# Block sums over two slots, packed rows for the rotary attention, and ScalarE writing the normalised rows, in a fused two-layer decoder

## The reference, cut to what matters

```
x = LN(x + taylor_attention(x));  x = LN(x + wide_cross_attention(x, ctx))      # layer 0
x = LN(x + gelu_experts(x))
x = LN(x + causal_attention(x))       # 16 heads of 8, softmax(q k / sqrt(8) + slopes) v, then Wo
x = LN(x + rotary_cross_attention(x, ctx))   # 16 heads of 8, q and k RMS-normed and rotated, 77 keys
x = LN(x + swiglu_experts(x))
```

## Time and profile before

| what | value |
|---|---|
| median of three runs | 2771.97 us |
| profiled execution | 2773.75 us |
| its trace's span | 2772.0 us |
| PE busy | 2534.0 us (91%) |
| DVE busy | 1904.9 us (69%) |
| ACT busy | 1671.0 us (60%) |
| POOL busy | 1694.9 us (61%) |
| DMA, one core's 16 engines | 97 GB/s mean |

### The profile page before, as it was taken

The page is one execution under the profiler, slowest core; times in us unless marked ns, Lnnn a source line. Parts: engine busy times, 40 slices in busy tenths (PEclk is TensorE's granted clock), DMA queues, the critical chain, the costliest instruction groups (busy, mean ns, idle before and its releaser), DMA issues. The chain is left out here.

```text
span 2772.0 us, 61590 instructions
## 1 busy us (share of the span) xinstructions
PE 2534.0 (91%) x19168; PEld 1864.5 (67%) x19168; DVE 1904.9 (69%) x5298; ACT 1671.0 (60%) x4543; POOL 1694.9 (61%) x2110
## 2 busy tenths in 40 slices
PE   8998999999999289996999999969999999699996
PEld 6665887877877289993555555547766666458993
DVE  6884677787777355555777777765788886445655
ACT  6773666666665234444766666639888887623334
POOL 3442334555555645554888888846688887724675
PEclk9998999999999699998999999979999999899998
DMA  8932467777774122214100000000011010011336
GB/s 260 338 107 68 151 215 226 234 224 224 223 220 129 54 65 71 72 58 129 58 11 9 9 11 9 7 25 13 16 30 30 30 30 17 30 30 54 93 93 194
DMA packets 274799, 267.86 MB, mean 97 GB/s; under 512 B 30060, under 2 KB 253561, under 8 KB 274096
## 3 DMA queue, kind: packets, MB, share of 16 engines
q1 hardware_dynamic: 256912, 228.42, 27.2%
q0 software_dynamic: 17280, 34.13, 3.6%
q10 hardware_dynamic: 288, 1.38, 0.2%
HBM read 101.24 MB, written 151.85 MB: 91 GB/s over the span
## 5 line engine op out<-in xcount | busy, mean ns | idle before, releaser
L779 POOL TENSOR_TENSOR wide_probs<-wide_exps,wide_inv_sum 128x616 f32<-128x616 f32 x128 | 168.3, 1315 | 305.6 <-DVE wide_inv_sum L1580 293.0
L749 POOL TENSOR_TENSOR causal_exps<-causal_biased,causal_neg_max 128x512 f32<-128x512 f32 x256 | 262.8, 1036 | 76.4 <-DVE causal_neg_max L1594 76.2
L758 POOL DMA_INDIRECT sorted_x<-send,place_i x240 | 244.1, 1017 | 84.2 <-ACT send L1233 44.0
L1289 ACT ACTIVATE rotary_exps<-banks,rotary_neg_max 128x77 f32<-128x77 f32 x1024 | 248.7, 341 | 19.3 <-DVE rotary_neg_max L1594 19.1
L1764 POOL DMA_INDIRECT results<-gelu_tile_out,gelu_dest_i x142 | 140.1, 986 | 142.2 <-DVE gelu_tile_out L1920 120.0
L1539 DVE TENSOR_TENSOR causal_biased<-banks,regions 128x512 f32<-128x512 f32 x256 | 163.6, 680 | 80.7 <-PE banks L1115 80.4
L1764 POOL DMA_INDIRECT results<-swiglu_tile_out,swiglu_dest_i x142 | 144.6, 1019 | 116.7 <-DVE swiglu_tile_out L1915 59.4
L1833 ACT ACTIVATE gelu_hidden<-banks,gelu_slot 128x256 f32<-128x256 f32 x284 | 116.6, 470 | 159.5 <-PE banks L2010 159.4
L1258 ACT ACTIVATE causal_exps<-causal_exps 128x512 f32<-128x512 f32 x256 | 161.2, 630 | 71.4 <-POOL causal_exps L749 71.4
L1594 DVE TENSOR_REDUCE rotary_neg_max<-banks 128x4 f32<-128x308 f32 x256 | 121.7, 475 | 113.5 <-PE banks L1129 105.1
L1273 ACT ACTIVATE causal_probsT<-banks 128x512 f32<-128x512 f32 x256 | 151.6, 592 | 79.3 <-PE banks L1140 79.3
(11 more groups left out here) (385 smaller groups left out, 7018.3 us busy)
## 6 DMA issues: line engine op xcount, KB each, us to landing
v_dram<-wide_staged SPq DMA_DIRECT2D x38, 1024.0 KB, 4.4
sorted_x<-blank SPq DMA_DIRECT2D x1, 34848.0 KB, 116.8
sorted_x<-blank SPq DMA_DIRECT2D x24, 1452.0 KB, 8.7
wide_folded<-v_dram SPq DMA_DIRECT2D x128, 256.0 KB
gelu_tile_in<-sorted_x SPq DMA_DIRECT2D x71, 132.0 KB, 2.1
swiglu_tile_in<-sorted_x SPq DMA_DIRECT2D x71, 132.0 KB, 2.1
gelu_back<-results SPq DMA_DIRECT2D x16, 512.0 KB, 8.0
swiglu_back<-results SPq DMA_DIRECT2D x16, 512.0 KB, 5.4
```

Source lines behind the costliest of these rows:

```text
L749: pool.tensor_tensor(exps[:, (NU * pair.c + m) % ES], biased[:, m % BS].rearrange("p (h n) -> p h n", h=HU), neg_max[:, m % SLOTS].unsquee ...
L758: pool.indirect_dma_start(route["sorted_x"], bass.IndirectOffsetOnAxis(ap=r_place_i[:, b % 2, which, n // 2:n // 2 + 1], axis=0), send[:, ...
L779: pool.tensor_tensor(probs[:, half % SLOTS, 0:HH * NK].rearrange("p (k h) -> p h k", h=HH), exps[:, half % EB], inv_sum[:, half % SLOTS].u ...
L1289: last = act.activation(exps[:, (NU * c.c + k) % ES, h], scores[:, h * NK:(h + 1) * NK], ACT.Exp, bias=neg_max[:, k % SLOTS, h:h + 1])
```

## The change

Line numbers in this section's order rows are those of the kernel they come from.

1. **Sums.** `late_sum`, four matmuls in each slot, becomes `late_sums` (causal) and `dense_sum` (rotary), eight matmuls in every second slot. In the causal stage the block stands right behind the score matmuls of even slots, PLAG is 5 instead of 4, and `probsT` has 4 buffers instead of 2.
2. **Rotary packed.** The exponentials of two slots (8 heads x 77 keys = 616 columns) lie side by side in a buffer of 640 columns. Five transposes of 128 columns take the place of eight of 77, and ACT copies 256 and 384 columns instead of 512 and 512. The values must then lie as 616 rows: they are made four pairs ahead (a third part of `early`), written by ACT to `v_rows` in SBUF, stored to DRAM by four DMAs and loaded to `v_dense` by five, for each pair. `v_rows` has one buffer; ACT waits until the store of the pair before has landed.
3. **Output chain.** In the causal stage the output transpose, copy and product come two to three slots later (OT_LAG 3, `turn_outputs` in slot 1 of the next step), the division in slots 5 and 6 instead of 4 and 6, and POOL adds the residual in slot 6 and makes `rstd` in slot 5.
4. **LN.** POOL computes shift = -mean x rstd (two instructions on 128x2), and ACT writes X as z x rstd + shift: two instructions of 128x128 a pair, in both stages, instead of DVE (causal) and POOL (rotary).
5. The context ring of the rotary stage has 4 buffers instead of 8.

```diff
-    FU = {"wide": 7, "causal": 4, "rotary": 2}[kind]
+    FU = {"wide": 7, "causal": 4, "rotary": 1}[kind]
-    EARLY = 2
+    EARLY = 3
+    PITCH, HALF_ROWS = 320, 8 * CONTEXT
-    OT, OT_LAG = (1, 1) if kind == "causal" else (2, 0)
+    OT, OT_LAG = (1, 3) if kind == "causal" else (2, 0)
...
+            def store_values(pair):
+                sp.wait_ge(early_done, pair.count(EARLY, EARLY))
+                rows = route["v_dram"][4 * HALF_ROWS * pair.c:4 * HALF_ROWS * (pair.c + 1)].rearrange("(m h k) c -> h k m c", h=4, k=NK)
+                for h in range(4):
+                    sp.dma_start(rows[h], v_rows[0:NK].rearrange("k (m r) -> k m r", r=PITCH)[:, :, 64 * h:64 * h + 64]
+                                 ).then_inc(v_stored, 16)
+            def load_values(pair):
+                s = pair.c % 2
+                sp.wait_ge(v_stored, 16 * 4 * (pair.c + 1))
+                if pair.c >= 2:
+                    sp.wait_ge(pv_done, pair.back(2).count(NU, NU))
+                for b in range(2):
+                    for n in range(2):
+                        at = HALF_ROWS * (2 * (2 * pair.c + b) + n)
+                        sp.dma_start(v_dense[:, s, b, n, 0:4], route["v_dram"][at:at + 512].rearrange("(c p) d -> p c d", p=P)).then_inc(v_loaded[s], 16)
...
-                    if c is not None and kind != "rotary" and k == 3:
+                    if c is not None and kind != "rotary" and k == (6 if kind == "causal" else 3):
...
-                    if n is not None and kind == "rotary" and k in (3, 4):
-                        pool.tensor_scalar(X[:, n.index(2, b), :], z[:, s, b], mean_var[:, s, b, 0:1], rstd[:, s, b:b + 1],
+                        if late:
+                            pool.wait_ge(rstd_done, n.count(1, 1))
+                            pool.tensor_tensor(shift[:, s], mean_var[:, s, :, 0], rstd[:, s], ALU.mult).then_inc(turned_done, 1)
+                            pool.wait_ge(turned_done, n.count(1, 1))
+                            pool.tensor_scalar(shift[:, s], shift[:, s], -1.0, None, ALU.mult).then_inc(shift_done, 1)
...
+            if m == 4:
+                if f.c >= 1:
+                    act.wait_ge(v_stored, 16 * 4 * f.c)
+                return act.activation(v_rows[0:NK].rearrange("p (m w) -> p m w", w=PITCH // 4)[:, :, 0:D],
...
-        EARLY_AT = [(0, 0), (1, 0)]
+        EARLY_AT = [(0, 0), (1, 0), (7, 0)]
-        TLAG, PLAG, OLAG = {"wide": (4, 5, 6), "causal": (3, 4, 5), "rotary": (2, 3, 4)}[kind]
+        TLAG, PLAG, OLAG = {"wide": (4, 5, 6), "causal": (3, 5, 5), "rotary": (2, 3, 4)}[kind]
+        DIVIDE_AT = (5, 6) if kind == "causal" else (4, 6)
...
+            def late_sums(pair, n):
+                b, g = n // UB, n % UB // 2
+                pe.wait_ge(probsT_done, pair.count(NU, n + 1))
+                for odd in range(2):
+                    for h in range(HU):
+                        last = pe.matmul(o_bank[b][32 * h:32 * h + 32, g * P:(g + 1) * P], values[:, pair.c % 2, strip:strip + 32],
+                                         probsT[:, (n - 1 + odd) % 4, h * P:(h + 1) * P], start=odd == 0, stop=odd == 1)
...
+            def dense_sum(pair, n):
+                b, g, s = n // UB, n // 2 % 2, pair.c % 2
+                pe.wait_ge(probsT_done, pair.count(NU, n + 1))
+                for second in range(2):
+                    for strip in range(4):
+                        chunk = strip + second
+                        last = pe.matmul(o_bank[b][32 * strip:32 * strip + 32, g * P:(g + 1) * P],
+                                         v_dense[:, s, b, g, chunk, 32 * (strip % 2):32 * (strip % 2) + 32],
+                                         probsT[:, (NU * pair.c + n) // 2 % 2, chunk * P:(chunk + 1) * P], start=second == 0, stop=second == 1)
...
+                    if kind == "rotary" and mine is not None and k == 4:
+                        s = mine.c % 4
+                        act.wait_ge(shift_done, mine.count(1, 1))
+                        for b in range(2):
+                            act.activation(X[:, mine.index(2, b), :], z[:, s, b], ACT.Identity, bias=shift[:, s, b:b + 1],
+                                           scale=rstd[:, s, b:b + 1]).then_inc(x_written, 1)
```

180 lines of the change are left out of this document (118 added, 62 removed).

## The result

| | before | after |
|---|---|---|
| median of the runs, us | 2770.5 (4 runs, 2765.8 to 2773.2) | 2740.0 (4 runs, 2739.0 to 2740.8) |
| ratio, 95% interval | | 0.9892 [0.9877, 0.9907] |
| profiled execution: span, us | 2772.0 | 2737.5 |
| mean granted TensorE clock | 0.957 | 0.956 |

A forecast was written before the change was run, and what follows sets the result against it. PE was taken to lead both stages, with POOL close in the causal one and all four engines close in the rotary one; 2773.75 - 45 (causal) - 45 (rotary) + 8 (warm-up) + 2 (chain end) = 2694 us, range 2650 to 2750.

The forecast's parts named there:

- Causal LN: Causal stage: POOL gains 0.54 us a pair, to 13.9; ACT's two copies, 0.32 each at most, are hidden.
- The "14.5": Causal stage: forecast period of a pair in us, a gain of 1.4 a pair, 45 us in all.
- The causal sums: Causal stage: four sum blocks instead of eight in a pair save 4 x 0.24 = 0.95 us of PE.
- Causal output chain: Causal stage: moving output transpose, residual and root removes PE's waits; nothing behind the moved work is late at the old pace.
- Both named waits: Causal stage, PE per pair: 0.32 us for an exponential and 0.53 us for the divided output; both would go.
- Rival A: Causal stage: POOL takes over; gain 0.5 us a pair, 16 us instead of 45, time 2723 us; chance 0.13.
- Rotary: 2.5 us less PE, period 15.2: Rotary stage: fewer sum blocks (1.2 us) and transposes (1.3 us) on PE; gain 1.4 us a pair, 45 us.
- Rival B: Rotary stage: DVE or ACT hold it; period 16.3 us, gain 10 us instead of 45, time 2729 us; chance 0.14.
- The extra gain that the prediction held possible from less work on POOL: Rotary stage: 1.6 us less POOL work shortens DVE's blocked time; gain nearer 2 than 1.4 us a pair, not counted.
- Values over DRAM: Rotary stage: values' store and load, 28 ns a packet (bounds 24 and 44), 8.6 us of a pair, hidden.
- rival C: Rotary stage: the values' store sets the pace, 2805 us, chance 0.07; a mild form, 2743 us, chance 0.06.
- Warm-up and chain end: Early rotary pairs wait for the previous store, 6.8 us a step: +8 us; longer chain at causal stage's end: +2 us.

## Why the prediction was wrong, point by point

- **Causal LN, the step that failed first.** "POOL gains two instructions on 128x2 ... ACT ... on 68% busy: hidden", and then a period between the totals of PE and POOL. The 0.54 us was the right size, but it was set against POOL's total. It stands between two subtractions on the loop and counts in full (15.5 to 15.0 without it). ACT's 32% of idle time hid nothing either: its two writes take 0.78 (0.32 each were taken from a copy), stand between two exponentials, and became the last link once the others were short (14.9 to 14.2 without them). The "14.5" was right for what the stage can do, 14.2, and wrong for where the work had been put.
- **The causal sums** came as far as the rows show: 0.12 us less behind each block, and PE's total is 1.3 lower, against 0.95 forecast; what a block costs in front was not measured. Of the 1.3, 0.6 arrived.
- **Causal output chain.** Both named waits went. "Behind the moved work nothing is late next" was wrong: root and shift now stand in front of the subtraction in slot 6, and PE waits 0.30 and 0.90 behind it. That is read from the timeline; of that block only the shift and the residual were moved by an experiment, not the root.
- **Rival A** had the right size, 0.5 a pair, and the engine. It is not POOL's load, which is 90% and not 97: load moved off the loop gave nothing.
- **Rotary: 2.5 us less PE, period 15.2.** In the first pairs PE's work fell by 2.0 (15.69 to 13.70) and the pair by 1.3, close to the forecast 1.4. The failing step is the window of 200 us in the earlier trace rows, an average over a pattern of four pairs in which one had DVE at 17.53 of 18.26 us. A saving on PE didn't move that pair; it was 18.3 and is 19.3, or 18.7 in other traces of the same code. Rival B had this mechanism, with DVE or ACT in PE's place, but a gain of 0.3 a pair; over the stage it is 0.7, and the difference comes from both ends of the stage, in part at a higher granted clock than before. The extra gain that the prediction held possible from less work on POOL didn't come: the multiply-add of the root took 0.51 us in the median before (L1370) and takes 0.74 after (L1472).
- **Values over DRAM, rival C.** Hidden, as forecast, with the packet at 18.5 ns, under the lower bound of 24; the DMA share is 0.44 and not 0.6. The rule on transfers under 512 bytes (the Trainium skill, DMA: Bandwidth & Descriptors, Specifications) names a read-modify-write; no price for one shows here. Per packet these are the cheapest, and per byte they cost 0.07 ns, between the context's 0.08 (308 bytes at 24 ns) and the 0.05 of X's rows (910 bytes on average at 44). Rival C's own sum doesn't follow from its terms: a stage that loses 32 and a warm-up of 30 give 2793, not 2805.
- **Warm-up and chain end.** +8 and +2 forecast; measured 4.5 (from the first early pair's squares, 1821.69 after and 1837.58 before, to the first exponentials, 29.8 against 25.3 us) and 4.0, together 8.5. The steps that wait for a store take 5.4 to 5.6 us, not 6.8, as the store lands within 5.2.
- **The range** held the time, because A and B were in it; that both would come together was not among the cases. By the prediction's own prices both together are 2773.75 - 16 - 10 + 8 + 2 = 2758, above the range. That 2740 lies inside is luck: each stage gained more than its rival said, 19.5 for 16 and 22.5 for 10.

## What to carry to other kernels

Where every pair has the same length and no engine is full, walk back over one pair, from an instruction that waited to what released it, until you meet the same instruction a pair earlier. The times then add up to the period whatever the way, so check that each link did wait for the one before it. Only work on that loop counts, however small, and work on an engine "with 30% idle" isn't hidden if it stands between two links. Look for a branch that runs beside the loop before expecting anything from cutting one. Judge a stage by single periods, not by an average window, when its work repeats over several, and compare pairs of the same place in the pattern at the same granted clock. The longest wait is not the bound if its removal only moves it.

## What the runs showed of the hardware

- A block of 32-column sum matmuls costs 0.58 us for eight and 0.35 for four to the next start: about 0.12 us fixed behind a block, if eight stream for twice as long as four, as estimated.
- Packets of 256 bytes, written to DRAM or read, 18.5 ns each on average (an estimate from the queue's total) at a DMA share of 0.44.
- Two instructions of POOL on 128x2 with a link between them cost 0.5 us of the queue; DVE does both in one.
- A new wait can cost clock besides its own length. In the run with the residual in slot 2, PE waited 0.80 us before 1503.40 and 0.89 before 1505.17; then the granted clock was 0.59 from 1506.0 to 1509.5, and PE's scores took 1.75 us in place of 1.13 (timeline of PE); in the run with the rows by DVE the granted clock of the causal window was 0.95, so part of it was at 1.2 GHz, where it is 1.00 after, all at 2.4. The kernel before has two such pairs at the end of the rotary stage, at 0.91 and 0.76.

```profile
1507.57 1.75 PE L1186 MATMUL banks<-causal_keys,causal_qT 64*128 64x512 f32 x4
```
